# A Mamba layer and a feed-forward layer: the slot's blocks laid out in a new order, first state on ACT, output by token rows

## The reference

```
u   = layernorm(x);  xn = rmsnorm(u) * norm_w
z, xBC, dt = split(xn @ in_proj)            # 2048 | 2048+512+512 | 32 columns
xBC = silu(causal_conv4(xBC) + conv_b)      # 4 taps in each channel
xs, B, C = split(xBC)                       # 32 heads of 64; B, C: 8 groups of 64
dt  = softplus(dt + dt_bias);  dA = exp(-dt * exp(A_log))
h_t = dA_t * h_(t-1) + (dt_t * xs_t) B_t    # per head, state 64 x 64
y_t = h_t . C_t + D * xs_t
g   = rmsnorm_by_group(y * silu(z)) * gate_norm_w
x   = x + u + g @ out_proj
x   = x + ffn(layernorm(x))                 # ternary weights, 128 -> 512 -> 128, gelu
```

## Time and profile before

| | us |
|---|---|
| median of 3 runs | 1144.25 (1142.11 to 1147.0) |
| profiled execution | 1145.73 |
| its span, first to last instruction | 1143.9 |

### The profile page before, as it was taken

How to read it: one execution, slowest core, us unless ns; L and a number is a source line. 1 busy time by engine, 2 the same in 40 slices (tenths; PEclk the granted TensorE clock), 3 DMA queues, 4 the chain that set the end, 5 groups by cost and what they waited for, 6 DMA issues and landing times.

```text
span 1143.9 us, 26227 instructions
## 1 busy us (share of the span) xinstructions
PE 1033.2 (90%) x8912; PEld 732.0 (64%) x8912; DVE 1059.9 (93%) x2004; ACT 970.0 (85%) x2836; POOL 868.6 (76%) x596
## 2 busy tenths in 40 slices
PE   1724789999999999999999999999999999996797
PEld 1603566676666666676666666766666666664576
DVE  7597999999999999999999999999999999989474
ACT  2767898999999999999999999999999999984464
POOL 7300356888888888888888888888888888885765
PEclk9955899999999999999999999999999999997899
DMA  6320000000000000000000000000000000021001
GB/s 170 117 86 0 10 1 2 1 1 2 1 30 2 2 2 29 2 2 2 29 2 2 2 29 2 2 2 29 2 1 1 21 1 2 1 78 46 1 29 46
DMA packets 28084, 22.58 MB, mean 20 GB/s; under 512 B 11696, under 2 KB 22576, under 8 KB 27824
## 3 DMA queue, kind: packets, MB, share of 16 engines
q1 hardware_dynamic: 25136, 20.90, 5.9%
q10 hardware_dynamic: 2816, 0.02, 0.1%
HBM read 12.78 MB, written 8.13 MB: 18 GB/s over the span
## 4 chain that ended last, share of the span: by engine, by line
PE 77%; DVE 14%; issue 3%; POOL 2%; ACT 2%; DMA 0%; POOLq 0%; DVEq 0%; ACTq 0%
PE bank L1713 10%; PE bank L1695 10%; PE bank L1625 8%; PE bank L1727 8%; PE bank L1641 8%; PE bank L1626 6%; PE bank L1627 6%; PE bank L1681 5%; PE bank L1662 5%; DVE conv L1191 4%; PE bank L1766 3%; PE bank L1738 2%; DVE lm L1181 2%; PE bank L1555 1%; PE bank L1746 1%
## 5 line engine op out<-in xcount | busy, mean ns | idle before, releaser
L1191 DVE SCALAR_TENSOR_TENSOR conv<-bank,cw,conv 128x509 f32<-128x509 f32 (+2 forms) x576 | 421.7, 743 | 16.6 <-ACT conv L762 8.6
L636 POOL TENSOR_TENSOR lm<-lm,cbs 128x1024 f32<-128x1024 f32 x128 | 304.3, 2377 | 75.7 <-ACT xw L866 75.7
L1181 DVE TENSOR_TENSOR_SCAN lm<-bank,ident 128x512 f32<-128x512 f32 x256 | 298.7, 1210 | 0.7 <-PE bank L1641 0.6
L911 ACT ACTIVATE xdt<-bank,dt_all 128x64 f32<-128x64 f32 x1024 | 222.3, 329 | 37.2 <-PE bank L1662 37.2
L866 ACT ACTIVATE xw<-xdt,lm 128x64 f32<-128x64 f32 x768 | 199.3, 365 | 0.0
L644 POOL TENSOR_TENSOR ssum<-ssum,sq 128x512 f32<-128x512 f32 x96 | 123.1, 1283 | 93.0 <-ACT sq L926 92.8
L1625 PE MATMUL bank<-xn_hi,w_hi 128*128 128x512 f32 x320 | 166.1, 519 | 13.8 <-DVE conv L1191 13.1
L615 POOL TENSOR_TENSOR gated<-gated,gate 128x512 f32<-128x512 f32 x128 | 164.9, 1288 | 15.9 <-DVE gated L1238 14.5
L626 POOL TENSOR_TENSOR gated<-gated,rbs 128x512 f32<-128x512 f32 x120 | 153.8, 1282 | 0.0
L877 ACT ACTIVATE conv<-bank,cb_bias,cw 128x512 f32<-128x512 f32 x189 | 142.6, 781 | 11.5 <-PE bank L1627 7.3
L1713 PEld LDWEIGHTS bank<-lm,xdt 128*64 128x64 f32 x2048 | 110.3, 137 | 63.7 <-issue 63.7
(11 more groups left out here) (217 smaller groups left out, 1766.5 us busy)
## 6 DMA issues: line engine op xcount, KB each, us to landing
lm<-in_L_attn_in_proj_w SPq DMA_DIRECT2D x1, 2048.0 KB, 11.7
xn_scratch<-chan SPq DMA_DIRECT2D x4, 512.0 KB, 4.6
r_stage<-residual_scratch SPq DMA_DIRECT2D x8, 256.0 KB, 2.9
xn_stage<-xn_scratch SPq DMA_DIRECT2D x7, 256.0 KB, 3.2
x_scratch<-r_stage SPq DMA_DIRECT2D x7, 256.0 KB, 2.0
gate<-in_L_attn_hidden_states SPq DMA_DIRECT2D x2, 512.0 KB, 4.6
cdec<-in_L_attn_hidden_states SPq DMA_DIRECT2D x2, 512.0 KB, 7.1
w_out<-in_L_attn_out_proj_w SPq DMA_DIRECT2D x8, 128.0 KB, 3.3
```

The lines of the kernel that those rows point to most:

```text
L636: gp.tensor_tensor(lm[:, mr, :, :], lm[:, mr, :, :], cbs[:, :, :], ALU.mult).then_inc(m_done, 1)
L911: act.activation(xdt[:, r, at:at + HP], misc_of("xt", n)[:, at:at + HP], ACT.Copy, scale=dt_h).then_inc(xdt_done, 1)
L1181: V.tensor_tensor_scan(lm[:, m % R, a, :], bc_bank[(3 * m + a) % 2][:, :], ident4[:, :], 0.0, ALU.mult, ALU.add).then_inc(scanned, 1)
L1191: V.scalar_tensor_tensor(out=conv[:, ci % 4, shift:S], in0=tile_bank(b, n, t)[:, 0:S - shift], scalar=cw[:, q, t, KW - 1 - shift:KW - shif ...
```

## The change

- **Banks of the shared plan:** in every kind "xt" comes before "s"; in kind 0 the two "cb" follow and then "var". The place of the output stays in the plan unused.
- **PE:** in all kinds the transposes come right after the tiles, the spread rows 2 and 0 early, then `inner` (states, y within, y from states in a row), then spread row 1. In kind 0, C times B, the first tile of the next slot (`next_tile`) and the variance follow; the kind-1 slot projects its second tile only. In kinds 1 and 2 the output product, in kind 1 also B and factor transposes, and the gate tile come after `inner`.
- **First state:** copied by ACT right after `scale_x` (`first_state`), no longer by DVE; DVE has two state steps a slot, and step 1 waits for ACT's copy.
- **pend:** all pairs and chunks are computed once by 16 small matmuls in slot 4 of the first batch and copied by DVE; no copy in each slot.
- **Root:** POOL expands the root itself, in slots of kind 1; ACT's `expand_root` goes. ACT copies the variance at the end of kind 0, after the start of the next slot's first tile.
- **Output:** for each of four chunks, the gated tokens are the weights and `w_out` the moving columns, so that the result is tokens by channels. DVE adds the bank to the residual rows right after the scans of slot 15 (`output_rows`); ACT's copy and PE's transposes go. The next batch's first output product waits for that addition (`x1_done`).
- **DVE's order:** taps, C product, then the steps, as in the diff. `dtb`, `alog`, `aexp` share the room of `qdiag`.

```diff
+def early_tile(b, n, t):
+    return n % R == 1 and t == PLAN[1][0] and (b, n) != (0, 1)
...
+            plan += [(n, "xt", LAG_SSD, 0), (n, "s", LAG_STATE, 0)]
             if r == 0:
-                plan.append((n, "var", LAG_VAR, 0))
...
+                plan += [(n, "cb", LAG_SSD, 0), (n, "cb", LAG_SSD, 1), (n, "var", LAG_VAR, 0)]
...
-        pend = sb("pend", [P, 4, CH])
+        pend = sb("pend", [P, SLOTS, NCH])
...
@@ POOL, root() @@
                     gp.tensor_tensor(rtok[:, :], vtok[:, :], neghalf[:, 0:2 * CH], ALU.pow).then_inc(rstd_done, 1)
+                    after(gp, rstd_done, UNITS, bb, v)
+                    after(gp, rbc_ready, UNITS, bb, v - 1)
+                    gp.tensor_copy(rexp[:, :, :], rtok[:, :].unsqueeze(2).broadcast_to([P, 2 * CH, HP])).then_inc(rexp_done, 1)
...
                 if r == 0:
                     decay_product()
                     normalise()
+                elif r == 1:
+                    normalise()
                     root()
+                    decay_product()
+                    square_sum()
...
@@ ACT @@
+                def first_state():
...
+                    bb, m = back(b, n, LAG_STATE)
+                    after(act, s_ready, SLOTS, bb, m)
+                    after(act, y_ready, SLOTS, bb, m - 2)
+                    act.activation(hpk[:, m % 2, 0, :], misc_of("s", n)[:, 0:NS], ACT.Copy).then_inc(hfirst, 1)
...
                     weigh()
                     convolve()
                     activate(0)
-                    copy_variance()
                     scale_x()
+                    first_state()
                     square()
                     gate_silu()
                     copy_cb()
+                    next_convolve()
+                    copy_variance()
                 elif r == 1:
                     convolve()
                     weigh()
                     activate(0)
-                    if not (b == NB and n == 9):
-                        expand_root(b, n)
                     scale_x()
+                    first_state()
                     square()
+                    copy_bt()
                     gate_silu()
-                    copy_bt()
                     copy_factor()
...
@@ DVE, state_step(c) @@
+                    if c == 1:
+                        after(dve, hfirst, SLOTS, bb, m)
...
+                        after(dve, hstep, 2 * SLOTS, bb, 2 * m + c - 2)
...
+                def output_rows():
...
+                    after(dve, out_step, SLOTS, bb, SLOTS - 1)
+                    dve.wait_ge(res_loaded, bb * 16 + 16)
+                    xs = r_stage[:, :, :]
+                    V.tensor_tensor(xs, out_bank[:, :].rearrange("p (c d) -> p c d", d=DM), xs, ALU.add).then_inc(x1_done, 1)
...
                 if ssd is not None:
                     scans()
+                output_rows()
                 if r == 0:
-                    taps(0, 1)
-                    state_step(0)
-                    taps(1, 2)
+                    taps(0, 3)
+                    chunk_ends()
                     state_step(1)
-                    taps(2, 3)
                     state_step(2)
+                elif r in (1, 2):
+                    taps(0, 3)
                     chunk_ends()
...
+                    taps(3, 4)
                     state_step(1)
...
                     taps(4, 5)
                     state_step(2)
                     taps(5, 6)
                 else:
-                    state_step(0)
-                    taps(0, 1)
+                    taps(0, 2)
                     chunk_ends()
-                    taps(1, 2)
+                    taps(2, 3)
                     state_step(1)
-                    taps(2, 3)
                     state_step(2)
...
@@ PE, out_product() @@
                     if m == 0:
-                        after(pe, out_copied, 1, bb, -1)
-                    last = MM(out_bank[:, :], w_out[:, m, :], gated[:, (m // R) % 2, m % R, :], start=(m == 0), stop=(m == SLOTS - 1))
+                        after(pe, x1_done, 1, bb, -1)
...
+                    for c in range(CH):
+                        tok = slice(P * c, P * c + P)
+                        last = MM(out_bank[:, tok], gated[:, (m // R) % 2, m % R, tok], w_out[:, m, :],
+                                  start=(m == 0 and c == 0), stop=(m == SLOTS - 1 and c == CH - 1))
...
@@ PE, order of the blocks, as it is after the change @@
+                def inner():
+                    states()
+                    y_within()
+                    y_states()
                 if r == 0:
                     out_product()
                     tiles()
                     transposes()
                     gate_tile()
                     rows(ssd, 2)
                     rows(ahead, 0)
+                    inner()
+                    rows(ahead, 1)
                     cb_products()
+                    next_tile()
+                    variance()
                 elif r == 1:
                     tiles()
                     transposes()
                     rows(ssd, 2)
                     rows(ahead, 0)
+                    inner()
+                    rows(ahead, 1)
+                    out_product()
                     b_transposes()
                     factor_transposes()
+                    gate_tile()
                 elif r == 2:
                     tiles()
                     transposes()
+                    rows(ssd, 2)
+                    rows(ahead, 0)
+                    inner()
+                    rows(ahead, 1)
                     out_product()
+                    gate_tile()
                 else:
                     tiles()
                     transposes()
                     out_product()
                     gate_tile()
                     rows(ssd, 2)
                     rows(ahead, 0)
+                    inner()
+                    rows(ahead, 1)
                     next_input()
...
@@ PE, once, after slot 4 of the first batch @@
+                    ends = pr_parts[:, :].rearrange("k (c i) -> k c i", i=P)[:, :, P - 1:P].rearrange("k c i -> k (c i)")
+                    for m in range(SLOTS):
+                        last = MM(out_bank[:, NCH * m:NCH * m + NCH], sel[:, m, HP:HP + P], ends, start=True, stop=True)
+                    last.then_inc(pend_ready, 1)
```

More of the change, by code:

```diff
@@ L872, in convolve, with begin @@
                     for t in PLAN[r]:
-                        ci = CONV_ORDER.index((q, t))
-                        after(act, proj_ready, NCONV, b, ci)
-                        after(act, silu_done, NCONV, b, ci - 4)
-                        act.activation(conv[:, ci % 4, :], tile_bank(b, n, t)[:, :], ACT.Identity,
-                                       scale=cw[:, q, t, KW - 1:KW], bias=cb_bias[:, q, t:t + 1]).then_inc(acc_init, 1)
+                        if not early_tile(b, n, t):
+                            begin(t, n)
+                def begin(t, n):
+                    ci = CONV_ORDER.index((q, t))
+                    after(act, proj_ready, NCONV, b, ci)
+                    after(act, silu_done, NCONV, b, ci - 4)
+                    act.activation(conv[:, ci % 4, :], tile_bank(b, n, t)[:, :], ACT.Identity,
+                                   scale=cw[:, q, t, KW - 1:KW], bias=cb_bias[:, q, t:t + 1]).then_inc(acc_init, 1)
                 def activate(k):
@@ L1298, in slot @@
                                     ALU.subtract).then_inc(lo_done, 1)
-                if n == XO_SLOT and back(b, n, SLOTS) is not None:
-                    bb, _ = back(b, n, SLOTS)
-                    after(dve, xo_ready, 1, bb, 0)
-                    dve.wait_ge(res_loaded, bb * 16 + 16)
-                    xs = r_stage[:, :, :]
-                    V.tensor_tensor(xs, misc_of("xo", n).rearrange("p (c d) -> p c d", d=DM), xs, ALU.add).then_inc(x1_done, 1)
             slot(0, 0)
@@ L1459, in _ @@
                 slot(0, n)
+                if n == R:
+                    dve.wait_ge(pend_ready, 1)
+                    V.tensor_copy(pend[:, :, :].rearrange("p m c -> p (m c)"), out_bank[:, :]).then_inc(pend_done, 1)
             for b in range(1, NB - 1):
@@ L1569, in misc_free @@
                     who = back(bb, pn, lag) if pkind != "xn" else following(bb)
-                    if who is not None:
+                    if who is not None and pkind != "unused":
                         break
@@ L1582, in misc_free @@
                 elif pkind == "s":
-                    after(pe, hstep, 3 * SLOTS, wb, 3 * wm + 2)
+                    after(pe, hstep, 2 * SLOTS, wb, 2 * wm + 1)
                 elif pkind == "var":
@@ L1587, in misc_free @@
                     after(pe, rbc_copied, UNITS, wb, wm // R)
-                elif pkind == "xo":
-                    xdt_there(pe, bb, pn - LAG_SSD)
-                    after(pe, x1_done, 1, wb, 0)
             def proj_free(b, i):
@@ L1667, in tiles, with next_tile @@
                         for t in PLAN[r]:
```

(49 more changed lines are left out.)

103 lines of the change are left out of this document (28 added, 75 removed).

## The result

The changed kernel took 1239.35 us (median of 4 runs), the kernel before 1145.57 beside it: ratio 1.0819, interval 1.0773 to 1.0866. The direction and the chain in kind 1 were as forecast, the size was not: 94 us where 57 were expected, and some of the steps priced at nothing were not free. The profiled execution took 1237.67 us.

What follows compares the result with a forecast made beforehand. The prediction took DVE as the bound. To 1145.7 us it added 46 (30 groups of four slots at +1.53), 10.5 for the residual, 3 for `pend`, less 1 at the end: 1204.2, given as 1203, range 1157 to 1231.

Steps and rivals of the forecast that it cites:

- the chain in kind 1: From DVE's step 2 of kind 0 through PE and ACT to the first state's copy: 8.40 us against DVE's 6.46.
- DVE is the bound: Before the change DVE works all but 0.33 us of every four slots; any DVE wait lengthens the kernel one for one.
- DVE's work after, 28.16: DVE's four slots: copies save 0.80 us, six chained pairs add 0.72, so 28.16 us in all.
- The price of a chained pair: A DVE instruction directly behind the one whose result it needs costs 0.11 to 0.12 us more.
- Kind 1 waits 1.94 for the first state: DVE's step 1 in kind 1 waits 1.94 us for ACT's copy, once in four slots.
- Kind 2 and the other kinds cost nothing: In kinds 0, 2 and 3 the first state comes in time: nothing, or up to 0.3 us each in kind 2.
- The margin of 0.4: Kind 2, from the bank-freeing tap to step 1: DVE has 6.8 us of work, PE and ACT need 6.4.
- Residual addition, 1.5 a time: Slot 15: PE's output product waits for DVE's addition, 0 to 2.9 us, taken as 1.5, seven times: +10.5 us.
- the fourth rival: PE, now with gaps, is given a lower clock: over 1232, up to 1310 us; chance 0.04.
- The end, -1: After the last batch, transposes and ACT's copy of the last output go: -1 us (0 to -1.3).
- First batch and `pend`: Start to batch 1: 6.1 us more, including 2 to 6, taken as 3, for filling `pend` once with DVE waiting.

Runs made afterwards that it cites:

- c6_var: c2_gate with the variance (and the last round's root) back in its old place, the end of kind 0: 1148.64 us, ratio 1.0043 to the kernel before.
- c5_var: c6_var with DVE's taps and steps of kinds 0 and 3 reordered, first state ahead of ACT's scalings there, so four chained pairs fewer: 1157.74 us, ratio 1.0134.
- s2_early: Changed kernel with ACT's copy of the first state directly behind the weighing in kinds 1 and 2, ahead of silu and scalings: 1204.22 us, ratio 1.0544.
- s6_var: Changed kernel with the variance alone, and with it the root, put back in the old place at the end of kind 0: 1211.6 us, ratio 1.0593.
- c2_gate: Changed kernel with s2_early's early copy, s3_res's early residual addition, and kind 1's gate tile and silu ahead of B's transposes and copy: 1163.2 us, ratio 1.0159.
- s3_res: Changed kernel with DVE's residual addition ahead of the two scans of slot 15 instead of behind them: 1223.08 us, ratio 1.0706.
- c4_tile: c2_gate plus c5_var's reordering, next slot's first tile and its start ahead of C times B and its copies, last root in kind 0: 1181.32 us, ratio 1.0299.

## Why the prediction was wrong

Of the 34 us by which the changed trace is longer than the sum, kind 2 makes 12 (28 groups of 0.42), kind 1 8 (28 of 0.27), the end 7, the clock 5 and the wait in slot 7 3, while kinds 0 and 3 give 1 back. So the steps that failed are kind 2 and the end, both put at nothing or less, and kind 1's chain was mis-sized. Term by term:

- **DVE is the bound**: only just not. PE's 115.44 was set aside as modelled, and it was the bound; DVE's own work was (113.5 - 1.2)/4 = 28.1, not 28.24. It explains why less work on DVE could not make the change faster by itself. For a loss on DVE it mattered little: after 0.5 us a group DVE sets the pace.
- **DVE's work after, 28.16**: right. With the waits out four slots took 28.35, of which 0.18 is a wait that is left. The price of a chained pair held: 0.12 in the loop. The Trainium skill, "VectorE: DVE Perf Modes", "The DRAIN you can't avoid", has such a semaphore for nothing; the runs here show otherwise, 0.24 us for two pairs in kind 3 (c6_var against c5_var).
- **Kind 1 waits 1.94 for the first state**: mechanism right (s2_early, s6_var), the slot 0.27 longer than summed. From step 2 of kind 0 to step 1 the chain took 8.69 (594.27 to 602.96) instead of 8.40: C times B starts 0.43 after that step, not 0.27, and ACT's start comes 0.98 after the second tile begins (597.49 to 598.47), not 0.81. Both are handings over from one engine to the next, which the sum had shorter.
- **Kind 2 and the other kinds cost nothing**: failed for kind 2, right for kinds 0 and 3. The margin of 0.4 was gone: 0.42 us (0.36 of it at step 1), where "up to 0.3" was allowed. The count began at the tap that frees the bank and left out what stands ahead of the starts on ACT, the gate's silu and the copy of the factor (605.60 to 606.57), held back through PE by kind 1's second step; c2_gate, which moves the gate tile, brings kind 2 to 7.88. With kind 1 this is 0.65 a group, some 16 of the 23 us missing in six batches.
- **Residual addition, 1.5 a time**: right, 1.55 in slot 15, and s3_res takes the same off a batch (126.22 to 124.67). That the middle of 0 to 2.9 was the value is luck. Not in the sum were the lower clock behind PE's wait in three of seven batches (2.6, 1.4 and 1.4 us more), the fourth rival on a small scale, and DVE's wait of 0.45 in slot 7.
- **The end, -1**: failed, +6.0. Only the transposes that go were counted. The moved variance puts the root one slot later, and in the last round GpSimd has the feed-forward layer's work ahead of it, so that PE waits 6.3 and 4.1 us for it. Taking that away gave between 1 and 6 us; the rest of the end is open.
- First batch and `pend`: 5.7 against 6.1, right.

## What to carry to other kernels

When two engines are within 2% of full, work taken from one gains at most the distance to the other (here nothing on DVE, 1.3% on PE), and a wait put on the other costs all that goes beyond that distance. Handing a short copy to another engine puts it into that engine's order: ask where in that order its input is ready, and what all the instructions ahead of it wait for, not how long the copy takes. And a step moved in the loop is moved in the last round too, where other work stands in the queue ahead of it.

## What was not expected of the hardware

In the changed kernel the granted clock fell to half after single PE waits of 2.2 us in slot 15, in three of seven batches; in s3_res, without that wait, it stayed at 1.00. In c4_tile it fell in ten places between 200 and 1000 us, one of them behind a wait of 0.77 us, of which there are 30 alike:

```profile
539.59 1.03 PE L1732 MATMUL bank<-blockones,ssum 128*128 128x2 f32 x8 [0.77 <-ACT cbs L984]
```

```profile
540.00:542.00 2.00, 2.00 (x12) 1.72 (x12) 1.19 (x2) 0.60 (x2) 2.00 (x2) 0.76 0.05 12
542.00:544.00 2.00, 2.00 (x19) 1.10 (x19) 1.53 (x3) 1.87 (x7) 1.94 (x3) 0.50 0.00 0
```

What tells such a wait from the others is open.
